# Moving a third of the local product and the last third of the gating to GpSimd, with output sums, scaling and MLP rows one to three rows later

## The chip, the cores and the metric

The kernel runs on one core of one Trainium2 chip. The metric is device time in microseconds (us), the median of three runs. The profile is one execution of the same program, recorded by the hardware profiler. PE is TensorE, DVE is VectorE, ACT is ScalarE, POOL is GpSimd, SP is the engine that only issues DMAs.

## What is computed

Eight samples of 384 channels on a 32 x 32 grid (1024 tokens) go through two layers. Cut to what matters:

```python
# layer 0, per sample
xn    = rmsnorm(x) * norm_w
u, z  = in_proj(xn)                      # mamba, forward and backward in time
u     = silu(causal_conv1d(u))           # 4 taps
dt, B, C = x_proj(u)
delta = softplus(dt_proj(dt))
h     = exp(delta * A) * h + delta * u * B    # scan over 1024 tokens, 16 states
y     = sum_n(h * C) + u * D             # both directions
g     = out_proj(y * silu(z)) * scale_mod
local = sigmoid(depthwise3x3(xn)) * xn
x     = x + res_scale * (g + local)
# layer 1, per sample
t = tokens(x)
t = t + Wo(causal_attention(layernorm(t)))    # 6 heads of 64
t = t + mlp(layernorm(t))                     # 384 -> 1536 -> 384, gelu
```

## The kernel before

Tensors are channel-major: three tiles (k = 0, 1, 2) of 128 channels x 1024 tokens. Layer 0 of sample b and layer 1 of sample b-1 are worked in the same iteration b; iterations 1 to 6 are one hardware loop, 0, 7 and 8 are written out. Iteration 8 has layer 1 alone.

**The head of an iteration.** PE makes the forward causal convolution in six halves (`causal`, L555), ACT applies SiLU to each half (`silu_u`, L895) between making the taps of the depthwise convolution for tile 2 (`tap_row_of`, L942 and L949; `TAPS` says how many taps come ahead of each SiLU), and POOL adds those taps (`depthwise`, L1495). DVE does the depthwise convolution of tiles 0 and 1 (L1268, L1272). PE then projects to dt, B and C (`steps_in`, L567), ACT copies the result out (`narrow_copies`, L855 and L856) and PE projects the step sizes (`step_size`, L603). ACT takes the three sigmoids (`gates`, L931, order `BRANCH` = tiles 0, 2, 1), DVE multiplies each by xn and `rs_col` (`local`, L1280), ACT does softplus (L868, L872, L876), DVE finishes it (L1239) and multiplies by u (L1256). POOL multiplies y by silu(z) of sample b-1, three tiles (`gated`, L1502), and PE's `out_project` (L512) waits for all three. Then PE makes z (`in_project`, L531).

**The rows.** 96 rows follow (r = 0 to 95: 2 directions x 16 states x 3 tiles). For each, POOL makes delta*u*B (`input_row`, L1521), ACT the decay (`decay`, L886, one row ahead), DVE the scan (`scan_row`, L1310) and the product with C (`output_row`, L1319), and POOL sums the result into y by an accumulating DMA, two rows later (`sum_row`, L1536). POOL also issues the local products to DRAM behind rows 0 to 2 (`keep_local`, L1507). PE is free of the rows and does the rest of both layers.

**The order of the rest** is written out by hand: `STEPS`, `FINISH`, `BEHIND` and `PLAN` give each item a row, and `SLOTS` collects the items of a row, in the order STEPS, FINISH, SOON, PLAN, rest of BEHIND. Every engine walks the same list and issues its part of each item in row r, in its own program order. On DVE an "early" part stands ahead of the row's scan and the other behind the row; on ACT, around the decay of row r+1. The items of the change are: `wo_add` (DVE adds the attention output to the residual, L1373), `next_*` (norm and input projection of sample b+1: L1144, L1407, L1412, L531, L969), `norm(1)` (L589, L1330, L1024), `mlp_raw` (ACT copies the reduced MLP input out of PSUM, L1106), `mlp_scale` (DVE scales it, L1393), `mlp_cast`, `mlp_split`, `mlp_low`, `mlp_fix` (splitting into bf16 parts, L1109 to L1113, L1396, L1399), `mlp` and `gelu` (four pairs a half, L765, L767, L782, L1121), `mlp_out` (L788, L791), `mlp_add` (ACT, L1134), and `step_silu` (ACT, SiLU of the backward convolution, L909, in row 17, where `PLAN` has attention projection 2, L1046). PE's projection n waits for ACT's copy of projection n-2. `finish` (DVE, rows 0 to 2, two each, L1302) takes the output of `out_project`. After row 95 ACT takes silu(z) of the sample (`silu_z`, L922).

In PE's program the six convolutions of the next head stand behind all items of row 95, so behind `mlp_out`; convolutions 1 to 3 also wait for `mlp_add`.

```python
elif kind == "wo":
    if n >= 2:
        pe.wait_ge(wo_add, at(6, a, n - 1))
```

Of the kernel before, what the change touches and what calls it, by code (L numbers as in the profile page):

```python
# [40 lines left out]
LAG = 2  # L41
TAPS = (0, 3, 3, 4, 5, 6, 6)
BRANCH = (0, 2, 1)
# [34 lines left out]
def norm(n, *rows):  # L78

    return list(zip(("ln_mean", "ln_xc", "ln_var", "ln_rs", "ln_apply"), [n] * 5, rows))  # L80
# [8 lines left out]
def attention():  # L89
# [7 lines left out]
    + [("ctx_t", t, S1 + t // 3) for t in range(6)] + [("wo", t, S1 + (1 if t < 2 else 3)) for t in range(6)]  # L97
    + [("wo_add", t, S1 + 3 + t // 2) for t in range(5)]
    + [("next_square", 0, S1 + 2), ("next_mean", 0, S1 + 2), ("next_rstd", 0, S1 + 4), ("next_norm", 0, S1 + 5), ("wo_add", 5, S1 + 5)]
    + norm(1, S1 + 5, S1 + 6, S1 + 7, S1 + 8)  # L100
    + [("next_in", t, S1 + (6, 8, 10)[t // 2]) for t in range(6)] + [("next_up", t, S1 + (7, 10, 12)[t // 2]) for t in range(6)]
    + [("mlp_in", 0, S1 + 7), ("mlp_raw", 0, S1 + 9), ("mlp_scale", 0, S1 + 10), ("mlp_cast", 0, S1 + 10),
       ("mlp_split", 0, S1 + 10), ("mlp_low", 0, S1 + 11), ("mlp_fix", 0, S1 + 11)] + mlp(0, S1 + 11) + mlp(1, S1 + 21), key=lambda x: x[2])
SOON = [x for x in BEHIND if x[0] in ("step_silu", "step_abs")]
SLOTS = [[(kind, n) for kind, n, row in STEPS + FINISH + SOON + PLAN + [x for x in BEHIND if x not in SOON] if row == r]
# [14 lines left out]
def hybrid_block(nc, x, chan, scal, k128, k32, w_in, w_x, w_dt, w_out, wq, wk, wv, wo, fc1, fc2, pr1, pr2, kept, bc_rows, out):  # L120
    with ExitStack() as ctx:
# [3 lines left out]
        def sem(name):  # L125
            return ctx.enter_context(nc.semaphore(name))
# [52 lines left out]
        def tiled(area):  # L179
# [57 lines left out]

        skip_added = sem("skip_added")
        da_ready, m1_done, scan_done, m2_done = (
            sem(n) for n in ("da_ready", "m1_done", "scan_done", "m2_done"))  # L240
# [255 lines left out]
        def _(pe):  # L496
# [95 lines left out]
            def step_size(b, d, k):  # L592

                g = KT * d + k
                pe.wait_ge(xd_evac, at(4, b, 2 * d + 2))
                if g < 3:
                    pe.wait_ge(m2_done, at(ROWS, b, 0))
                if g == 2:
                    pe.wait_ge(loc_ready, at(KT, b, BRANCH.index(1) + 1))
                if g > KT:  # L600
                    pe.wait_ge(delta_ready, at(6, b, g))
                for c in range(2):
                    mm = pe.matmul(dt_bank[g][:, c * HALF:(c + 1) * HALF], dt_w[d][:, 128 * k:128 * k + 128],  # L603
                                   dtr[d][:, c * HALF:(c + 1) * HALF], start=True, stop=True)
                mm.then_inc(dt_ready, 1)
# [235 lines left out]
        def _(act):  # L841
# [82 lines left out]
            def gates(b, lo, hi):  # L924

                for k in BRANCH[lo:hi]:
                    if k < VK:
                        act.wait_ge(dw_step, at(9 * VK, b, 9 * (k + 1)))
                    else:
                        act.wait_ge(tap_added, at(8, b, 8))  # L930
                    act.activation(taps[k], taps[k], ACT.Sigmoid).then_inc(sig_ready, 1)  # L931

# [217 lines left out]
            def iteration(b, layer0, layer1, more):  # L1150
                if layer0:
# [27 lines left out]
                    for k in range(2):  # L1179
                        skip(b, 0, k)  # L1180
                    for r, d, n, k in rows():
                        for kind, i in beside(r, layer1, more):
                            item(kind, i, b, True)
                        if r + 1 < ROWS:
                            decay(b, r + 1)
                        for kind, i in beside(r, layer1, more):
                            item(kind, i, b, False)
# [10 lines left out]
        def _(dve):  # L1198
# [76 lines left out]
            def local(b, k):  # L1275

                dve.wait_ge(sig_ready, at(KT, b, BRANCH.index(k) + 1))
                for i in range(KT):
# [54 lines left out]
            def item(kind, n, b, early):  # L1333
# [67 lines left out]
                elif kind == "next_norm" and not early:  # L1401
# [7 lines left out]
                    dve.wait_ge(rstd_ready, at(1, b + 1, 1))  # L1409
                    dve.wait_ge(loc_ready, at(3, b + 1, 0))  # L1410
                    for k in range(KT):
# [6 lines left out]
            def iteration(b, layer0, layer1, more):  # L1418
                if layer0:
# [5 lines left out]
                    if b == 0:  # L1425
                        split_hidden()
                    for k in BRANCH:
                        local(b, k)
# [29 lines left out]
        def _(pool):  # L1458
# [37 lines left out]

            def gated(b):

                for k in range(KT):
                    pool.wait_ge(y_in[k], at(YIN, b, YIN))  # L1500
                    pool.wait_ge(zs_ready, at(3, b, k + 1))
                    pool.tensor_tensor(zs[:, k, :], y[:, k, :], zs[:, k, :], ALU.mult).then_inc(yz_ready, 1)  # L1502

            def keep_local(b, k):

                pool.wait_ge(loc_ready, at(KT, b, BRANCH.index(k) + 1))
                pool.dma_start(kept[b][128 * k:128 * k + 128, :], gate[k], accum_op=ALU.add).then_inc(kept_add[k], 16)  # L1507
# [40 lines left out]
            def iteration(b, layer0, layer1, more):  # L1548
                if layer0:
                    depthwise(b)  # L1550
                    if layer1:
                        gated(b - 1)
                    pool.wait_ge(kept_set, at(16, b, 16))
                    for r in range(ROWS):
                        for kind, i in beside(r, layer1, more):
                            item(kind, i, b, more)
                        input_row(b, r)
                        if r < KT:
                            keep_local(b, (1, 0, 2)[r])
# [72 lines left out]
```

## Time and profile before

| | |
|---|---|
| median of three runs | 4047.45 us (4042.24 to 4050.1) |
| the profiled execution's own time | 4031.18 us |
| its span, first to last instruction | 4029.3 us |
| PE busy | 3381.3 us, 84% |
| DVE busy | 3497.5 us, 87% |
| ACT busy | 2597.6 us, 64% |
| POOL busy | 2817.5 us, 70% |
| mean granted TensorE clock | 0.894 of full speed |

The busy shares are means over stages: a head (from the last product of row 95 to the scan of row 0, some 37 us) and the 96 rows have different limits. What a moved item costs is read from the stage where it stands.

### The profile page before, as it was taken

The page shows a single profiled execution, that of the slowest core. Times are in us where ns is not written, and L with a number is a line of the kernel's source. Part 1 is how long each engine was busy: PE and PEld are TensorE (multiplying, and loading weights), DVE is VectorE, ACT ScalarE, POOL GpSimd, SP SyncE. Part 2 cuts the span into 40 slices and gives each one's busy share as a digit, 9 for nine tenths or more (in the row PEclk, how much of TensorE's full clock was granted, in tenths as well). Part 3 has the DMA queues.
Part 4 walks back from the last instruction along what each step waited for, and adds up shares of the span by engine and source line. Part 5 has one row for each costly group of instructions (what it writes and reads, how often), then busy time and mean ns, then how long its engine had stood idle before and what let it go on. Part 6 is the DMA issues. An engine that isn't in the chain of part 4 may idle for free.

```text
span 4029.3 us, 39801 instructions
## 1 busy us (share of the span) xinstructions
PE 3381.3 (84%) x11706; PEld 1712.9 (43%) x11722; DVE 3497.5 (87%) x2671; ACT 2597.6 (64%) x3599; POOL 2817.5 (70%) x1714
## 2 busy tenths in 40 slices
PE   7504589988899898989899888998989898996999
PEld 2101236623374235733366234742357333651473
DVE  6999999999899998999999998999999999999121
ACT  5533567676676757767676766767577666767363
POOL 3889887687866877678866888668776788668000
PEclk8756699989999899988999899988999889997999
DMA  4999797898978988888978988789988889789000
GB/s 105 233 249 247 194 230 181 205 211 217 213 186 194 233 210 191 191 205 212 230 185 200 222 210 213 186 194 227 216 187 192 209 210 223 184 196 229 6 7 16
DMA packets 220548, 770.79 MB, mean 191 GB/s; under 512 B 24908, under 2 KB 40574, under 8 KB 220062
## 3 DMA queue, kind: packets, MB, share of 16 engines
q0 software_dynamic: 113616, 413.71, 53.2%
q1 hardware_dynamic: 106702, 354.32, 26.4%
q8 instruction: 107, 1.75, 0.2%
q14 instruction: 123, 1.01, 0.1%
HBM read 339.60 MB, written 39.85 MB: 94 GB/s over the span
## 4 chain that ended last, share of the span: by engine, by line
PE 43%; DVE 20%; issue 12%; ACT 9%; DMA 9%; POOL 7%; ACTq 0%; DVEq 0%; POOLq 0%
DVE pB L1310 14%; PE pW L711 9%; PE pW L624 9%; DMA y<-hb 9%; POOL hb L1521 5%; PE pW L589 4%; PE pW L512 4%; PE pW L555 3%; PE pW L640 3%; ACT pt L1068 2%; PE pW L567 2%; DVE hb L1319 2%; PE pW L782 1%; PE pW L531 1%; PE pW L739 1%
## 5 line engine op out<-in xcount | busy, mean ns | idle before, releaser
L1310 DVE TENSOR_TENSOR_SCAN pB<-pB,hb 128x1024 f32<-128x1024 f32 x768 | 1757.0, 2288 | 67.4 <-ACT pB L886 59.8
L1536 POOL DMA_DIRECT2D y<-hb x765 | 750.1, 980 | 610.6 <-DVE hb L1319 553.8
L1521 POOL TENSOR_TENSOR hb<-du_f,b_row 128x1024 f32<-128x1024 f32 x384 | 1001.0, 2609 | 128.1 <-DMA y<-hb 72.5
L1521 POOL TENSOR_TENSOR hb<-uc_b,b_row 128x1024 f32<-128x1024 f32 x384 | 993.0, 2587 | 72.8 <-DMA y<-hb 68.8
L1319 DVE TENSOR_TENSOR hb<-pB,c_row 128x1024 f32<-128x1024 f32 x768 | 940.2, 1224 | 45.1 <-DVE pB L1310 0.9
L886 ACT ACTIVATE pB<-delta,vec 128x1024 f32<-128x1024 f32 x384 | 429.1, 1118 | 306.2 <-DVE hb L1319 291.4
L886 ACT ACTIVATE pB<-xres,vec 128x1024 f32<-128x1024 f32 x384 | 428.6, 1119 | 213.3 <-DVE hb L1319 212.6
L711 PE MATMUL pW<-area,pt 128*128 128x64 f32 x3456 | 438.0, 281 | 19.3 <-ACT pt L1068 11.7
L711 PEld LDWEIGHTS pW<-area,pt 128*128 128x128 f32 x3456 | 410.6, 195 | 69.1 <-ACT pt L1068 59.0
L1357 DVE TENSOR_REDUCE stat<-pW 128x1 f32<-128x640 f32 (+7 forms) x361 | 258.6, 753 | 161.9 <-PE pW L627 161.9
L1078 ACT ACTIVATE prob<-pW,stat 128x640 f32<-128x640 f32 (+7 forms) x361 | 266.5, 748 | 27.7 <-DVE stat L1357 27.7
L531 PE MATMUL pW<-area,xn_area 128*128 128x512 f32 x576 | 261.7, 610 | 22.1 <-DVE area L1412 10.0
L1068 ACT COPY pt<-pW 128x512 f32<-128x512 f32 x378 | 216.2, 587 | 81.1 <-PE pW L640 75.7
L624 PE MATMUL pW<-area,v_w 128*128 128x512 f32 (+3 forms) x540 | 223.8, 539 | 45.8 <-ACT prob L1078 28.1
L782 PE MATMUL pW<-du_f,pr_w 128*32 128x512 f32 x384 | 223.5, 730 | 29.2 <-ACT du_f L1121 29.2
L555 PE MATMUL pW<-area,v_w 128*128 128x512 f32 x512 | 235.4, 617 | 12.8 <-ACT uc_b L902 5.0
L640 PE MATMUL pW<-consts,prob 128*128 128x128 f32 x1512 | 227.5, 282 | 16.0 <-ACT xn_area L977 15.4
L977 ACT ACTIVATE xn_area<-pW,stat 128x64 f32<-128x64 f32 x384 | 102.5, 311 | 191.6 <-DVE stat L1368 139.7
L624 PE MATMUL pW<-area,w_ko 128*128 128x512 f32 (+3 forms) x542 | 209.5, 509 | 0.2
L640 PEld LDWEIGHTS pW<-consts,prob 128*128 128x128 f32 x1512 | 164.5, 144 | 105.5 <-issue 100.1
L589 PE MATMUL pW<-area,consts 128*128 128x512 f32 x192 | 90.4, 621 | 137.3 <-ACT area L1140 136.2
L1495 POOL TENSOR_TENSOR prob<-prob,hb 128x1024 f32<-128x1024 f32 x64 | 152.4, 2381 | 62.1 <-ACT hb L949 56.1
(185 smaller groups left out, 4953.9 us busy)
## 6 DMA issues: line engine op xcount, KB each, us to landing
y<-hb POOLq DMA_DIRECT2D x765, 512.0 KB, 7.6
b_row<-bc_rows SPq DMA_DIRECT2D x256, 512.0 KB, 5.8
c_row<-bc_rows SPq DMA_DIRECT2D x256, 512.0 KB, 5.7
du_f<-in_x SPq DMA_DIRECT2D x8, 1536.0 KB, 13.1
kept_residual<-in_x SPq DMA_DIRECT2D x8, 1536.0 KB, 20.8
xres<-kept_residual SPq DMA_DIRECT2D x8, 1536.0 KB, 15.7
out_x<-xa SPq DMA_DIRECT2D x7, 1536.0 KB, 8.5
kept_residual<-hb POOLq DMA_DIRECT2D x16, 512.0 KB, 5.3
```

Source lines behind the costliest of these rows:

```text
L531: mm = pe.matmul(bank, ip_w[:, k, 128 * m:128 * m + 128], xnp[:, k, 1 + 16 * c:17 + 16 * c, 1:1 + WW], start=(k == 0), stop=(k == KT - 1))
L555: mm = pe.matmul(pW[:, 2 + i % 2 if d else (i + 3) % 4, :], cd[m][:, 128 * j:128 * j + 128], up[:, m, off:off + HALF], start=(j == 0), sto ...
L624: pe.matmul(bank[:, lo:hi], q, kT[:, h // 2, lo - c0:hi - c0], start=True, stop=hi != end)
L640: mm = pe.transpose(prob_bank(b, half)[:, 128 * j:128 * j + 128], prob[:, half * HALF + 128 * j:half * HALF + 128 * j + 128], ident)
L711: mm = pe.matmul(value_bank(b, g)[:, DH * t:DH * t + DH], pt[:, col:col + 128], vtok[:, j, DH * h:DH * h + DH], start=(m == 0 and q == 0), ...
L886: act.activation(pBC[r % 2][:, :], delta[d][:, k, :], ACT.Exp, scale=vec[:, k, V_A + n:V_A + n + 1]).then_inc(da_ready, 1)
L1068: act.copy(pt[:, half * HALF:(half + 1) * HALF], prob_bank(b, half)).then_inc(pt_ready, 1)
L1078: ex = act.activation(prob[:, c0:end], scores_bank(b, n)[:, c0:end], ACT.Exp, bias=stat[:, 0, st:st + 1], accum_out=stat[:, 1, st:st + 1])
L1310: dve.tensor_tensor_scan(flow(d, buf), flow(d, buf), flow(d, hb[r % NHB][:, :]), 0.0, ALU.mult, ALU.add).then_inc(scan_done, 1)
L1319: dve.tensor_tensor(hb[r % NHB][:, :], pBC[r % 2][:, :], c_row[g % 2][:, :], ALU.mult)\
L1521: pool.tensor_tensor(hb[r % NHB][:, :], du[d][:, k, :], b_row[g % 2][:, :], ALU.mult)\
L1536: pool.dma_start(y[:, k, :], hb[r % NHB][:, :], accum_op=ALU.add).then_inc(y_in[k], 16)
```

## The change

- One third of the local product moves. ACT's sigmoid of tile 2 signals `gate_ready`, ACT scales it by `rs_col` behind the first two skip products (a new 128 x 1024 Identity), and POOL multiplies it by xn in row 2, ahead of its `keep_local` DMA. DVE does tiles 0 and 1 only.
- One third of the gating moves. POOL gates tiles 0 and 1 where it did, and tile 2 behind `input_row` of row 0.
- Taps and SiLUs: `TAPS` puts two taps ahead of the first SiLU instead of three, and one tap more behind the last.
- `step_silu` leaves `SOON`, so that in row 17 it stands behind attention projection 2.
- Rows: `wo_add` 0 to 5 from rows 64, 64, 65, 65, 66, 66 to 64, 64, 66, 66, 67, 67; `next_norm`, `norm(1)`, `next_in`, `next_up`, `mlp_in` and `mlp_raw` one row later; `mlp_scale` to `mlp_fix` and the first MLP half two rows later; the second MLP half three rows later, so that its last GELU is in row 92, `mlp_out` in 93 and `mlp_add` in 95.

```diff
-TAPS = (0, 3, 3, 4, 5, 6, 6)
+TAPS = (0, 2, 2, 3, 3, 4, 5)
...
-    + [("wo_add", t, S1 + 3 + t // 2) for t in range(5)]
-    + [("next_square", 0, S1 + 2), ("next_mean", 0, S1 + 2), ("next_rstd", 0, S1 + 4), ("next_norm", 0, S1 + 5), ("wo_add", 5, S1 + 5)]
-    + norm(1, S1 + 5, S1 + 6, S1 + 7, S1 + 8)
-    + [("next_in", t, S1 + (6, 8, 10)[t // 2]) for t in range(6)] + [("next_up", t, S1 + (7, 10, 12)[t // 2]) for t in range(6)]
-    + [("mlp_in", 0, S1 + 7), ("mlp_raw", 0, S1 + 9), ("mlp_scale", 0, S1 + 10), ("mlp_cast", 0, S1 + 10),
-       ("mlp_split", 0, S1 + 10), ("mlp_low", 0, S1 + 11), ("mlp_fix", 0, S1 + 11)] + mlp(0, S1 + 11) + mlp(1, S1 + 21), key=lambda x: x[2])
-SOON = [x for x in BEHIND if x[0] in ("step_silu", "step_abs")]
+    + [("wo_add", t, S1 + (3, 3, 5, 5, 6)[t]) for t in range(5)]
+    + [("next_square", 0, S1 + 2), ("next_mean", 0, S1 + 2), ("next_rstd", 0, S1 + 4), ("next_norm", 0, S1 + 6), ("wo_add", 5, S1 + 6)]
+    + norm(1, S1 + 6, S1 + 7, S1 + 8, S1 + 9)
+    + [("next_in", t, S1 + (7, 9, 11)[t // 2]) for t in range(6)] + [("next_up", t, S1 + (8, 11, 13)[t // 2]) for t in range(6)]
+    + [("mlp_in", 0, S1 + 8), ("mlp_raw", 0, S1 + 10), ("mlp_scale", 0, S1 + 12), ("mlp_cast", 0, S1 + 12),
+       ("mlp_split", 0, S1 + 12), ("mlp_low", 0, S1 + 13), ("mlp_fix", 0, S1 + 13)] + mlp(0, S1 + 13) + mlp(1, S1 + 24), key=lambda x: x[2])
+SOON = [x for x in BEHIND if x[0] == "step_abs"]
...
-                    act.activation(taps[k], taps[k], ACT.Sigmoid).then_inc(sig_ready, 1)
+                    act.activation(taps[k], taps[k], ACT.Sigmoid).then_inc(sig_ready if k < VK else gate_ready, 1)
...
                     for k in range(2):
                         skip(b, 0, k)
+                    act.wait_ge(gate_ready, at(1, b, 1))
+                    act.activation(taps[VK], taps[VK], ACT.Identity, scale=rs_col).then_inc(gate_scaled, 1)
...
-                    for k in BRANCH:
+                    for k in range(VK):
                         local(b, k)
...
-            def gated(b):
+            def gated(b, lo, hi):
 
-                for k in range(KT):
+                for k in range(lo, hi):
...
             def keep_local(b, k):
 
-                pool.wait_ge(loc_ready, at(KT, b, BRANCH.index(k) + 1))
+                if k < VK:
+                    pool.wait_ge(loc_ready, at(VK, b, k + 1))
+                else:
+                    pool.wait_ge(gate_scaled, at(1, b, 1))
+                    pool.tensor_tensor(gate[k].rearrange("p (h w) -> p h w", w=WW),
+                                       gate[k].rearrange("p (h w) -> p h w", w=WW),
+                                       xnp[:, k, 1:1 + HH, 1:1 + WW], ALU.mult).then_inc(loc_last, 1)
+                    pool.wait_ge(loc_last, at(1, b, 1))
...
-                        gated(b - 1)
+                        gated(b - 1, 0, 2)
...
                         input_row(b, r)
+                        if r == 0 and layer1:
+                            gated(b - 1, 2, 3)
```

The remaining lines of the diff adapt the counts that `local`, `step_size` and `next_norm` wait for; `next_norm` also waits for `loc_last`, since it overwrites xn.

## Rows read from the trace of the kernel before

**Rows 1.** The chain that ended last, iterations 2 to 3: start, duration, what.

```profile
1359.60 1.46 ACT du_f L1121
...
1371.60 22.58 PE pW L555 x48
...
1394.94 5.37 PE pW L567 x12
```

**Rows 2.** DVE timeline: scans of rows 92 and 95, and of row 0.

```profile
1367.51 2.29 DVE L1310 TENSOR_TENSOR_SCAN pB<-pB,hb 128x1024 f32<-128x1024 f32 x1
...
1377.97 2.29 DVE L1310 TENSOR_TENSOR_SCAN pB<-pB,hb 128x1024 f32<-128x1024 f32 x1
...
1418.54 2.29 DVE L1310 TENSOR_TENSOR_SCAN pB<-pB,hb 128x1024 f32<-128x1024 f32 x1
```

**Rows 3.** ACT timeline: end of iteration 2 and head of 3.

```profile
1371.14 1.44 ACT L1134 COPY xa<-pW 128x1536 f32<-128x1536 f32 x1 [2.39 <-PE pW L791]
...
1400.34 1.00 ACT L855 COPY pt<-pW 32x1024 f32<-32x1024 f32 x1 [3.26 <-PE pW L567]
...
1423.38 1.12 ACT L886 ACTIVATE pB<-delta,vec 128x1024 f32<-128x1024 f32 x1 [1.63 <-DVE delta L1239]
```

**Rows 4.** POOL timeline in the head of iteration 3.

```profile
1405.92 8.01 POOL L1502 TENSOR_TENSOR zs<-y,zs 128x1024 f32<-128x1024 f32 x3
1415.18 2.36 POOL L1521 TENSOR_TENSOR hb<-du_f,b_row 128x1024 f32<-128x1024 f32 x1 [1.25 <-DVE du_f L1256]
```

**Rows 5.** PE timeline: the output projection of iteration 3.

```profile
1414.35 18.41 PE L512 MATMUL pW<-zs,w_qp 128*128 128x512 f32 x36
```

**Rows 6.** Stretches of PE: length, busy and records, granted clock, DMA share, GB/s.

```profile
1418.00:1420.00 2.00, 2.00 (x4) 0.55 0.61 86
```

**Rows 7.** DVE timeline: the first pair of `finish`, iteration 3.

```profile
1424.46 1.40 DVE L1302 SCALAR_TENSOR_TENSOR xa<-pW,tiny,xres 128x512 f32<-128x512 f32 x2
```

**Rows 8.** PE and DVE timelines around rows 17 to 22.

```profile
1485.46 10.46 PE L512 MATMUL pW<-xn_area,w_qp 128*128 128x512 f32 x24
1498.82 4.27 PE L512 MATMUL pW<-xn_area,w_qp 128*128 128x512 f32 x6 [2.90 <-ACT area L1046]
...
1499.81 2.30 DVE L1310 TENSOR_TENSOR_SCAN pB<-pB,hb 128x1024 f32<-128x1024 f32 x1 [1.90 <-ACT pB L886]
...
1516.01 2.30 DVE L1310 TENSOR_TENSOR_SCAN pB<-pB,hb 128x1024 f32<-128x1024 f32 x1 [5.64 <-ACT pB L886]
```

**Rows 9.** DVE timeline: the stall of row 22 in iterations 2 and 6.

```profile
1044.67 2.30 DVE L1310 TENSOR_TENSOR_SCAN pB<-pB,hb 128x1024 f32<-128x1024 f32 x1 [3.86 <-ACT pB L886]
...
2924.03 2.30 DVE L1310 TENSOR_TENSOR_SCAN pB<-pB,hb 128x1024 f32<-128x1024 f32 x1 [6.83 <-ACT pB L886]
```

**Rows 10.** DVE timeline: stalls in the second half of iteration 2.

```profile
1255.90 0.75 DVE L1373 SCALAR_TENSOR_TENSOR xa<-pW,vec,xa 128x512 f32<-128x512 f32 x1 [0.55 <-PE pW L512]
1258.48 0.75 DVE L1373 SCALAR_TENSOR_TENSOR xa<-pW,vec,xa 128x512 f32<-128x512 f32 x1 [1.82 <-PE pW L512]
...
1287.27 0.69 DVE L1393 TENSOR_TENSOR pW<-prob,pW 128x512 f32<-128x512 f32 x1 [1.59 <-ACT prob L1106]
1289.21 0.70 DVE L1393 TENSOR_TENSOR pW<-prob,pW 128x512 f32<-128x512 f32 x1 [1.25 <-ACT prob L1106]
...
1343.12 2.30 DVE L1310 TENSOR_TENSOR_SCAN pB<-pB,hb 128x1024 f32<-128x1024 f32 x1 [1.83 <-ACT pB L886]
```

**Rows 11.** Waits of DVE over the span: us in total, times, longest.

```profile
DVE pB L1310 <- ACT pB L886: 59.8, 29, 6.8
...
DVE pW L1393 <- ACT prob L1106: 19.2, 14, 1.6
```

**Rows 12.** ACT, POOL and PE timelines at the end of iteration 7.

```profile
3718.50 2.95 ACT L922 ACTIVATE zs<-zs 128x1024 f32<-128x1024 f32 x3
...
3719.70 2.36 POOL L1546 TENSOR_TENSOR zs<-y,zs 128x1024 f32<-128x1024 f32 x1 [1.24 <-ACT zs L922]
...
3728.78 15.74 PE L512 MATMUL pW<-zs,w_qp 128*128 128x512 f32 x30 [16.22 <-DVE zs L1293]
```

More of the change, by code:

```diff
@@ L238, in hybrid_block @@
         skip_added = sem("skip_added")
+        gate_ready, gate_scaled, loc_last = sem("gate_ready"), sem("gate_scaled"), sem("loc_last")
         da_ready, m1_done, scan_done, m2_done = (
@@ L598, in step_size @@
                 if g == 2:
-                    pe.wait_ge(loc_ready, at(KT, b, BRANCH.index(1) + 1))
+                    pe.wait_ge(loc_ready, at(VK, b, VK))
                 if g > KT:
@@ L1275, in local @@
             def local(b, k):
-                dve.wait_ge(sig_ready, at(KT, b, BRANCH.index(k) + 1))
+                dve.wait_ge(sig_ready, at(VK, b, k + 1))
                 for i in range(KT):
@@ L1409, in item @@
                     dve.wait_ge(rstd_ready, at(1, b + 1, 1))
-                    dve.wait_ge(loc_ready, at(3, b + 1, 0))
+                    dve.wait_ge(loc_ready, at(VK, b + 1, 0))
+                    dve.wait_ge(loc_last, at(1, b + 1, 0))
                     for k in range(KT):
```

## The prediction

> **What bounds the kernel now.** The page's busy shares are near each other for DVE and PE and name no bound, so I read the chain of waits first, then the timelines of iteration 2 into 3 (the others repeat them), then DVE's waits. In the rows DVE sets the pace: a row takes (1377.97 - 1367.51) / 3 = 3.49 us [rows 2], and moving an item helps there only where it removes a DVE stall. In the head it is otherwise. The chain goes from the last GELU of the MLP through its reduction and `mlp_out` straight into the six convolutions, 22.58 us of PE without a break, then `steps_in`, the copies and softplus [rows 1]. ACT stands idle 3.26 us until `steps_in` ends [rows 3]. So whatever starts the convolutions later makes the head longer by as much, and what starts them is the end of the MLP, since PE's program has them behind it.
>
> **MLP rows.** The last GELU moves from row 89 to 92: three rows, 3 x 3.49, 10.4 us. It stands behind a decay as before, so it starts at 1370.0 instead of 1359.60 and the convolutions at 1382 instead of 1371.60 [rows 1], half a us past the end of row 95 at 1381.5 (its scan from 1377.97, one row long [rows 2]). Nothing on the way has slack, since ACT waited for PE already [rows 3]. ACT gets `mlp_add`, silu(z) and the taps later too; I place its last taps but one at 1410, just when `steps_in` is due. `TAPS` as changed fits that and gives nothing in these heads, where the SiLUs wait for PE. Six heads (2 to 7) follow an iteration with an MLP and convolutions behind it: 6 x 10.4 = **+62.4**. Bounds: 0, if the head had another bound, and 66, if the taps come 0.6 late. In heads 0 and 1 no MLP is in the way and convolution 4 waits for the first SiLU, which now has one tap less ahead of it, about 1.1 us each (the decay of the same shape took 1.12 [rows 3]): **-2**.
>
> At the end of iteration 7 the copy of `mlp_add`, 1.44 us [rows 3], runs after row 95 (3723.0), and silu(z) behind it. With a table load and the first SiLU, 2.4 us, POOL's first gating starts at 3726.9 instead of 3719.70, 7.2 later; from there to `out_project` it was 9.1 us [rows 12]. Some of the 9.1 was DVE's own last product, which no longer waits, so I take **+6**, between 4 and 8.
>
> Late with it is the load of the residual that `finish` reads, issued behind the output store. It has over 30 us in heads 2 to 7 and 15 at the end, and I give it nothing. The Trainium skill, Trainium Kernel Development and Optimization, Key Constraints, says that DMAs issued from the SP, ACT and POOL queues run on the same 16 DMA engines and interleave. By it the store and the load, issued together now, share bandwidth, and the last head could wait some us for them; no row shows the two side by side.
>
> **The later third of the gating.** Three gatings took 8.01 us and ended at 1413.93; `out_project` began at 1414.35. POOL's first input row ended at 1417.54 [rows 4, 5]. The third gating now follows that: 1417.54 + 2.36 = 1419.9, and `out_project` starts 5.55 us later. It makes six results of six records. The first six records run at half clock, to about 1419.8 [rows 6]; the other 30 take (18.41 - 5.45) / 30 = 0.43 each, 2.58 a result. PE stands idle ahead of it, so I assume the same slow start: results at 1425.0, 27.6, 30.2, 32.8, 35.4 and 38.0. DVE took them in pairs, without waiting, at 1424.46 [rows 7] and then every 4.8 us (a row and the pair). Now the second result holds it 2.6 us, and the fourth and sixth about 0.4 each: **3.5** a head, seven heads (1 to 7), **+24.5**. Bounds: nothing, if PE is quick, and 5.55 each, 39 in all. z follows 5.5 us later; its copies in rows 4 to 7 are then just in time.
>
> **The local third.** DVE loses a product of 1.3 us a head, but it waited between these products for ACT, so the chain gains nothing. ACT's new scaling, about 1.1 us, fits ahead of decay 1, where ACT idled 1.63 us [rows 3]; without that gap it would be on the path of row 1, 8 us in all, kept for the range. POOL's new product, 2.36 us by the nearest row [rows 4], comes in row 2. Input rows 3 to 5 come 2 to 3 us later by it, and `sum_row` and the DMAs queued behind it on POOL too; DVE, 3.5 us late, still finds them ready. So 0; if DVE is not late, some 1 us a head.
>
> **`step_silu` behind projection 2.** Four projections run from 1485.46 in 10.46 us, so projection 2 is ready at 1493.3; its copy comes only behind the SiLUs and two table loads, and it is what lets PE go on at 1498.82, slower than before [rows 8]. `steps_in` and the copies that precede the decay of row 22 follow, and DVE stalls 5.64 us. Now the copy comes at 1493.4, ahead of the SiLUs. PE goes on at 1495.9 and reaches `steps_in`'s end some 4.4 us sooner; in exchange the decay of row 19 is 1.0 us later, 0.8 of it ACT waiting for the projection. The stalls 1.90 and 5.64 [rows 8] become 2.9 and 0.4: -4.2 here. The seven stalls of row 22 lie between 3.86 and 6.83 [rows 9] and make 36.2 of the 59.8 in DVE's waits for the decay [rows 11]. Less 7 x 1.0 for row 19 and 7 x 0.4 left: **-26**. Bounds: +7 (only the later decay) and -36.
>
> **Output sums, scaling, second MLP half.** DVE waits 0.55 + 1.82 = 2.37 us for the third and fourth output sum [rows 10], in other iterations 3.6. A row later both are ready; 0.35 is left at `next_norm`. Iterations 1 to 6 together -17, 7 another -1: **-18**. `mlp_scale` waits 1.59 + 1.25 = 2.84 us for ACT's copies [rows 10], 19.2 in all [rows 11]. A row of distance more ends that wait. But `next_up` 2 and 3 now stand ahead of `mlp_cast` on ACT and wait for PE, which starts on them with ACT's copies at 1288.5 and needs 2 x 2.58 us: cast at 1294.3, and `mlp_split` waits for it, 1.4 us. **-10**. The first GELU of the second half stalls DVE by 1.83 us, one row behind `mlp_add` [rows 10]; two rows behind it does not. Five such stalls and small ones of 0.2: **-11**, within the same 59.8 [rows 11]. Bounds for the three: -20 and -52.
>
> **The sum.** 62.4 - 2 + 6 + 24.5 - 26 - 18 - 10 - 11 = **+26 us**. Against the profiled execution (4031.2 us, of which 4029.3 are span) that is 4057. The median of the runs shown is 16 us above it, and I add to the median: 4047.45 + 26 = 4073.5. About 0.2%, 8 us, is what a measurement of this kernel can tell from no change.
>
> **Rivals.**
> - *The row-17 gain does not come*: the backward chain or ACT keeps row 22 late. For: ACT's copies, decays and SiLUs of rows 17 to 21 stand in one queue, and I placed them. Against: both the stall and PE's gap of 2.90 ahead of it are rows [rows 8]. 26 + 26 to 33 = +52 to +59, about 4103.
> - *The later gating costs next to nothing*: 26 - 24.5 = +1.5, and with the sums' and the scaling's waits gone entirely -3; about 4048. For: PE may start faster than I assume. Against: 5.55 us against a slack of 3.
> - *The late MLP is absorbed*, the other side. Place: the start of the convolutions. It decides if the head is not waiting for them: if `steps_in` could end 10 us later and the copies on ACT not move. Then 62.4 and 6 fall away: 26 - 68 = -42, 4005; with half absorbed -8. For: ACT has much other work in the head. Against: ACT's wait of 3.26 us and the chain itself [rows 1, 3].
> - *It doesn't do what it says*: the rows are fixed lists, so little can fail. 0.02.
>
> **Chances.** Forecast (+10 to +42) 0.46; no row-17 gain 0.20; gating free 0.18, half of it within 0.2% and a quarter on each side; MLP absorbed 0.14, of which 0.02 within 0.2%; the last 0.02, within. Faster by over 0.2%: 0.045 + 0.12, about 0.16; within 0.09 + 0.02 + 0.02 = 0.13; slower 0.71. The range, 4042 to 4108, holds the first two cases and most of the third, and leaves out the absorbed one.
>
> **What would show it.** Right: the convolutions of heads 2 to 7 start half a us behind row 95, not 10 us ahead of its end; from the scan of row 95 to that of row 0 it is 40.57 [rows 2] + 10.4 = 51.0; L1302 stands among DVE's waits with about 3.5 us a head; row 22 stalls under 1 us; L1373 and L1393 nearly leave the waits and L1396 enters with 1.4. Wrong: the convolutions start late and the head keeps its length, or stalls appear in rows 82 to 95.

## The result, and the profile after

The changed kernel takes 4058.5 us against 4040.8 for the kernel before (medians of 20 runs each): 17.7 apart. The ratio is 1.0039, interval 1.0031 to 1.0047, so 12.5 to 19 us slower. The forecast was 4073.5, +26 on a median of 4047.45; that median of three runs lay 6.6 us above the one of 20.

The profiled executions lie further apart than the medians: spans 4029.3 and 4061.4 us, 32 apart. That of before took 4031.2 us, 9.6 below the median of its kernel; that of after took 4063.2, 4.7 above the median of its own. So 14 of the 32 us come from which executions were profiled. Part of it has a place: in three iterations of before rows 17 to 23 take 26.8 us, where the five runs below that leave `step_silu` in place need 28.4 or more in 34 of 35 iterations, and 5 to 9 us more over seven. All differences of segments below are against that trace of before.

The page of after, its head and busy times:

```profile
span 4061.4 us, 39821 instructions
...
PE 3389.5 (83%) x11722; PEld 1716.3 (42%) x11722; DVE 3481.0 (86%) x2663; ACT 2605.6 (64%) x3607; POOL 2835.6 (70%) x1722
```

DVE has 16 us less work, POOL 18 more, ACT 8 more, and the mean granted clock is 0.886 instead of 0.894. None of these shares tells the sign. The waits of DVE do (us in total, times, longest):

```profile
DVE hb L1283 <- ACT pB L932: 88.9, 15, 16.5
DVE xa L1305 <- PE pW L513: 42.5, 33, 8.9
...
DVE xa L1376 <- PE pW L513: 21.0, 7, 11.1
DVE pB L1313 <- ACT pB L887: 18.1, 16, 1.5
DVE pB L1313 <- POOL hb L1532: 16.1, 25, 2.1
...
DVE pW L1399 <- ACT pt L1110: 1.5, 6, 0.3
```

(L1283, L1305, L1313, L1376 and L1399 were L1280, L1302, L1310, L1373 and L1396. Of L1376's 21.0 all but 0.8 lie in iteration 8, which has no rows.) The wait for the decay fell from 59.8 to 18.1 and L1393's 19.2 left the list [rows 11]. In exchange DVE waits 88.9 us for the first sigmoid of a head, 14.9 before, and 42.5 for `out_project`, 13.6 before. With the starts of the 768 scans in DVE's timeline the span falls into segments; this table sums them (us, after minus before):

| segment | change | term of the prediction |
|---|---|---|
| heads 2 to 7 | +58.4 | MLP late, +62.4 |
| head 1 | -1.4 | taps, -2 with head 0 |
| rows 0 to 3, iterations 1 to 7 | +32.4 | later gating, +24.5 |
| rows 17 to 23 | -37.1 | `step_silu`, -26 |
| rows 23 to 33 | +8.7 | none |
| rows 61 to 76 | -32.2 | sums and scaling, -28, and part of the next |
| rows 76 to 87 | -10.1 | second MLP half, -11 |
| behind the last scan | +7.1 | +6 |
| iteration 0 and other rows | +6.3 | 0 |

**The head.** ACT's timeline of iteration 2 into 3 (start, duration, what, idle ahead and its releaser):

```profile
1372.25 1.45 ACT L1122 ACTIVATE du_f<-pW 128x1536 f32<-128x1536 f32 x1
...
1383.68 1.44 ACT L1135 COPY xa<-pW 128x1536 f32<-128x1536 f32 x1 [3.95 <-PE pW L792]
...
1412.32 1.00 ACT L856 COPY pt<-pW 32x1024 f32<-32x1024 f32 x1 [0.80 <-PE pW L568]
```

PE's timeline, the same head:

```profile
1380.81 2.84 PE L792 MATMUL pW<-narrow,mixed 32*128 32x512 f32 x6
1383.58 15.70 PE L556 MATMUL pW<-area,v_w 128*128 128x512 f32 x32
1399.12 7.03 PE L556 MATMUL pW<-area,w_ko 128*128 128x512 f32 x16
1406.92 5.36 PE L568 MATMUL pW<-area,xp_w 128*56 128x512 f32 x12 [0.78 <-ACT area L896]
```

and DVE's:

```profile
1380.35 2.29 DVE L1313 TENSOR_TENSOR_SCAN pB<-pB,hb 128x1024 f32<-128x1024 f32 x1
...
1417.87 1.28 DVE L1283 SCALAR_TENSOR_TENSOR hb<-pB,tiny,area 128x1024 f32<-128x1024 f32 x1 [10.28 <-ACT pB L932]
...
1428.97 1.75 DVE L1259 TENSOR_TENSOR du_f<-delta,area 128x1024 f32<-128x1024 f32 x1
1430.64 2.28 DVE L1313 TENSOR_TENSOR_SCAN pB<-pB,hb 128x1024 f32<-128x1024 f32 x1
...
1438.63 0.75 DVE L1305 SCALAR_TENSOR_TENSOR xa<-pW,tiny,xres 128x512 f32<-128x512 f32 x1 [1.39 <-PE pW L513]
1441.21 0.75 DVE L1305 SCALAR_TENSOR_TENSOR xa<-pW,tiny,xres 128x512 f32<-128x512 f32 x1 [1.82 <-PE pW L513]
```

Count from the scan of row 95. The last GELU stands 8.1 us ahead of it (8.0 predicted), the convolutions start 3.2 behind it (4.0 predicted; before, they started 6.4 ahead of it [rows 1, 2]), and row 0 follows at 1430.64 - 1380.35 = 50.29 us (51.0 predicted). In this head everything behind the convolutions moved rigidly: they are 9.6 us later and row 0 is 9.7 later. ACT's wait for `steps_in` shrank from 3.26 [rows 3] to 0.80, since its last taps but one came late as well, but PE's `steps_in` still ended it.

Over heads 2 to 7 the convolutions start 10.6 us later on the mean, and the way from them to row 0 is 0.9 shorter, 46.5 us for 47.3; together they make the 58.4. The time was won mostly in heads 5 and 7. There, before, the convolutions had started 8.9 us or more ahead of the scan of row 95, and PE stood still among them for 1.2 and 2.4 us, waiting for ACT's SiLU (L895). Row 0 came 48.8 and 50.0 us behind their start; in the changed kernel, where nothing interrupts them, it is 46.7 and 46.6.

**The gating.** POOL's timeline in the same head:

```profile
1427.28 2.35 POOL L1532 TENSOR_TENSOR hb<-du_f,b_row 128x1024 f32<-128x1024 f32 x1 [4.73 <-DVE du_f L1259]
1429.59 3.33 POOL L1506 TENSOR_TENSOR zs<-y,zs 128x1024 f32<-128x1024 f32 x1
```

PE's timeline, the output projection behind it:

```profile
1433.16 18.30 PE L513 MATMUL pW<-zs,w_qp 128*128 128x512 f32 x36 [6.88 <-POOL zs L1506]
```

The stretches of its start (length, busy and records, granted clock, DMA share, GB/s):

```profile
1433.00:1435.00 2.00, 1.84 (x2) 0.50 0.47 39
1435.00:1437.00 2.00, 2.00 (x4) 0.50 0.97 182
1437.00:1439.00 2.00, 2.00 (x4) 0.64 1.00 143
1439.00:1449.00 10.00, 10.00 (x25) 1.00 0.91 186
```

After 6.88 us of idleness PE starts at a granted clock of 0.50, the lower level, 1.2 GHz, as assumed. The kernel before started this projection without idling, and the clock stood no higher:

```profile
1414.00:1416.00 2.00, 2.00 (x3) 0.50 0.00 0
1416.00:1418.00 2.00, 2.00 (x4) 0.50 0.00 0
```

The first result is there 5.5 us after the start, the next 2.58 later. DVE stalls 1.39 us for the first, 1.82 for the second and 0.28 each for the fourth and the sixth; the prediction had 2.6 for the first pair and 0.4 each. The third gating took 3.33 us, not 2.36; `out_project` starts 2.52 us behind the scan of row 0, where before it started 4.19 ahead [rows 2, 5]: 6.7 later, not 5.55.

The seven heads have 25.6 us of these stalls, 3.7 each, close to the 3.5 predicted. The rest of the +32.4 is mostly work that got longer. In row 0 DVE's third product of delta and u now runs beside POOL's input row of row 1, which the late gating pushed there, and takes 1.82 us (1.47 in iteration 1) where it took 1.22; a pair of finishes, now taken singly, takes 0.1 us more:

```profile
1435.42 1.82 DVE L1259 TENSOR_TENSOR du_f<-delta,area 128x1024 f32<-128x1024 f32 x1
```

**Row 17.** ACT's timeline in iteration 3; the first line is its copy of attention projection 2:

```profile
1508.84 0.67 ACT L1047 ACTIVATE area<-pW,tiny 128x512 f32<-128x512 f32 x1
1509.52 1.28 ACT L910 ACT_TABLE_LOAD   x1
1510.82 2.95 ACT L910 ACTIVATE uc_b<-uc_b 128x1024 f32<-128x1024 f32 x3
1513.78 1.28 ACT L1002 ACT_TABLE_LOAD   x1
1515.08 1.12 ACT L887 ACTIVATE pB<-delta,vec 128x1024 f32<-128x1024 f32 x1
```

PE's timeline there:

```profile
1500.75 11.75 PE L513 MATMUL pW<-xn_area,w_qp 128*128 128x512 f32 x27
1513.82 5.36 PE L568 MATMUL pW<-uc_b,xp_w 128*56 128x512 f32 x12 [1.32 <-ACT uc_b L910]
```

DVE's scan of row 19:

```profile
1516.23 2.30 DVE L1313 TENSOR_TENSOR_SCAN pB<-pB,hb 128x1024 f32<-128x1024 f32 x1 [1.49 <-ACT pB L887]
```

The 5.64 us of row 22 are gone, in all seven iterations, and the stall of row 19 fell from 1.90 [rows 8] to 1.49, where 2.9 was expected (over seven iterations from 11.8 to 10.4 us).

### The profile page after: what moved, and what is told of

The parts are those of the page before. It is cut to its first block, busy times and chain, and to the rows that moved or that the text cites. A ratio compares the mean times of both kernels' runs of the same rounds, so it can differ in the third digit from the quotient of the medians.

```text
span 4061.4 us, 39821 instructions
## 1 busy us (share of the span) xinstructions
PE 3389.5 (83%) x11722; PEld 1716.3 (42%) x11722; DVE 3481.0 (86%) x2663; ACT 2605.6 (64%) x3607; POOL 2835.6 (70%) x1722
## 3 DMA queue, kind: packets, MB, share of 16 engines
q0 software_dynamic: 113616, 413.71, 52.8%
q8 instruction: 106, 1.74, 0.2%
## 4 chain that ended last, share of the span: by engine, by line
PE 46%; DVE 23%; issue 12%; ACT 8%; POOL 6%; DMA 5%; ACTq 0%; DVEq 0%; POOLq 0%
DVE pB L1313 17%; PE pW L712 10%; PE pW L625 9%; PE pW L513 7%; DMA y<-hb 5%; PE pW L556 4%; POOL hb L1532 4%; PE pW L590 3%; PE pW L641 3%; ACT pt L1069 2%; PE pW L532 2%; DVE hb L1322 2%; PE pW L568 1%; PE pW L783 1%; PE pW L604 1%
## 5 line engine op out<-in xcount | busy, mean ns | idle before, releaser
L1313 DVE TENSOR_TENSOR_SCAN pB<-pB,hb 128x1024 f32<-128x1024 f32 x768 | 1757.1, 2288 | 34.9 <-ACT pB L887 18.1
L1532 POOL TENSOR_TENSOR hb<-du_f,b_row 128x1024 f32<-128x1024 f32 x384 | 1013.1, 2640 | 98.5 <-DVE du_f L1259 45.3
L1079 ACT ACTIVATE prob<-pW,stat 128x640 f32<-128x640 f32 (+7 forms) x361 | 266.1, 747 | 27.7 <-DVE stat L1360 27.7
L625 PE MATMUL pW<-area,v_w 128*128 128x512 f32 (+3 forms) x540 | 226.8, 545 | 37.6 <-ACT prob L1079 25.6
```

The lines of the kernel that those rows point to most:

```text
L625: pe.matmul(bank[:, lo:hi], q, kT[:, h // 2, lo - c0:hi - c0], start=True, stop=hi != end)
L1313: dve.tensor_tensor_scan(flow(d, buf), flow(d, buf), flow(d, hb[r % NHB][:, :]), 0.0, ALU.mult, ALU.add).then_inc(scan_done, 1)
L1532: pool.tensor_tensor(hb[r % NHB][:, :], du[d][:, k, :], b_row[g % 2][:, :], ALU.mult)\
```

## The experiments

All ratios are to the kernel before. Where us stand beside a ratio, they are the ratio's difference from 1 times 4040.8.

### The rows: late MLP alone, all rows alone, all but the rows

```diff
# e1_late_half: before, with
-    ... + mlp(0, S1 + 11) + mlp(1, S1 + 21)
+    ... + mlp(0, S1 + 11) + mlp(1, S1 + 24)
# e5_rows_only: before, with the whole PLAN of after
# e4_rows_back: after, with the whole PLAN of before
```

> The kernel before with one edit: the second half of the MLP starts at row 85 instead of 82 (last GELU in row 92). Theory A (the end of the MLP starts the convolutions, and the head waits for them): heads 2 to 7 are 10 us longer, the end of iteration 7 is 6 us longer, and the first GELU of the second half no longer stalls DVE (-10 us): +52 to +58 us, ratio about 1.013 to 1.014. Theory B (the late MLP is absorbed by other work of the head): heads as before, 0 to -10 us, ratio 0.998 to 1.000.

> The kernel before with all row moves of the plan and nothing else. Theory A (the late second half costs what it did alone, and the sums and the scaling give back their waits): +51 from the late half, -17 to -24 from the sums and the scaling, that is +27 to +34 us, ratio 1.0067 to 1.0085, as the difference of the changed kernel and the rows-back one (28). Theory B (the parts work on each other): below +15 or above +45.

> The changed kernel with the rows of the plan (output sums, norm, scaling, MLP) as they were before; gating, local third, taps and the SiLU behind projection 2 stay. Theory A (the late end of the MLP is the loss of the change): against the kernel before, later gating +24 to +32, row 17 -26 to -37: -10 to +5 us, ratio 0.997 to 1.001, so 15 to 25 us faster than the changed kernel. Theory B (the rows pay for themselves): slower than the changed kernel, +20 us or more against the kernel before.

The late second half alone: ratio 1.0126 (1.0107 to 1.0145), +51 us, one below the 52 to 58 of Theory A, with the interval across it. Heads 2 to 7 grow by 52.8, the end by 4.7, and rows 76 to 87 give 8.3 back. Among DVE's waits, behind the attention's line, stands now:

```profile
DVE hb L1280 <- ACT pB L931: 65.8, 7, 12.1
```

All rows alone: 1.0059 (1.0045 to 1.0072), +24 (18 to 29); Theory A had 27 to 34. Heads 2 to 7 +53.1, end +7.1, rows 61 to 87 -42.8. The other way round, after with the old rows: 0.9977 (0.9967 to 0.9987), below the kernel before, and 25 us below after by the ratios, 27.7 by the medians. So the rows cost 24 to 28 us; the prediction's row terms make 62.4 + 6 - 18 - 10 - 11 = 29.4. The convolutions do wait for the end of the MLP, and the rival in which the late MLP is absorbed is refuted.

### The gating: alone, taken back, and behind the products

```diff
# e2_late_gating: before, with gated(b, lo, hi) as in after, and
-                        gated(b - 1)
+                        gated(b - 1, 0, 2)
...
                         input_row(b, r)
+                        if r == 0 and layer1:
+                            gated(b - 1, 2, 3)
# e7_gating_back: after, with these lines undone
# e10_gating_waits: e2_late_gating, with
                         if r == 0 and layer1:
+                            pool.wait_ge(du_ready, at(6, b, 2))
                             gated(b - 1, 2, 3)
```

> The kernel before with one edit: POOL gates the third tile behind the first input row. Theory A (out_project is late by the third gating plus the input row): DVE waits at the finishes, 3.5 us a head by the prediction's placing, 4.6 by the trace after, in seven heads: +24 to +32 us, ratio 1.006 to 1.008. Theory B (part of the 4.6 us of rows 0 to 3 comes from POOL's new product and not from the gating): +10 to +20 us.

> The kernel after, with all three gatings back in the head of the iteration; the late rows, step_silu behind projection 2 and the local third stay. Theory A (every term of the prediction stands on its own wait, so they add): the kernel before with late gating alone lost 33 us, the kernel after with the rows back lost 25 us by its late gating, so this gains 25 to 33 on the kernel after: 4026 to 4034, ratio to the kernel before 0.996 to 0.998. Rows 0 to 3 take 16.8 us again, the finish line's wait for out_project is back to some 14 us in all, the heads 2 to 7 stay at 48 to 51 us. Theory B (late MLP and late gating overlap in the head, so that each hides part of the other): under 15 us of gain, 4044 or more. Theory C (they make each other worse): over 40 us of gain, under 4018.

> The later gating alone, with one more wait: POOL's third gating waits for DVE's second product of delta and u, and so cannot run beside it. Theory A (3.33 us of that gating instead of 2.36 is the two instructions keeping each other from SBUF): the third gating takes 2.36 us, starts about 1 us later and ends when it did, so the time is that of the later gating alone, 4074, within 5 us. Theory B (the 3.33 us have another cause, such as the DMAs in flight): the gating still takes 3.3 us, ends 1 us later and the kernel is 6 to 7 us slower, 4080.

Alone: 1.0087 (1.0070 to 1.0104), +35 (28 to 42), above the 24 to 32 of Theory A. Rows 0 to 3 grow by 27.5, the predicted place, and rows 23 to 33 by 11: there DVE waits 14.7 us for ACT's softplus (L876), against 4.0 before. Taken back from after: 0.9985 (0.9975 to 0.9995), 22 us below after by the ratios, 25.8 by the medians (4032.7), at the edge of Theory A. There rows 0 to 3 shrink by 32.0, while rows 3 to 17 grow by 6.0, of which below.

The third run asks why the gating takes 3.33 us. It lets it wait until DVE's second product of delta and u is done. POOL's timeline about the scan of row 0 in iteration 4, with the late gating alone (e2):

```profile
1903.82 2.35 POOL L1521 TENSOR_TENSOR hb<-du_f,b_row 128x1024 f32<-128x1024 f32 x1 [3.22 <-DVE du_f L1256]
1906.13 3.33 POOL L1502 TENSOR_TENSOR zs<-y,zs 128x1024 f32<-128x1024 f32 x1
```

The same with the wait (e10):

```profile
1916.06 2.34 POOL L1502 TENSOR_TENSOR zs<-y,zs 128x1024 f32<-128x1024 f32 x1 [1.16 <-DVE du_f L1256]
```

DVE's timeline beside them in e2:

```profile
1905.52 1.74 DVE L1256 TENSOR_TENSOR du_f<-delta,area 128x1024 f32<-128x1024 f32 x1
1907.18 2.29 DVE L1310 TENSOR_TENSOR_SCAN pB<-pB,hb 128x1024 f32<-128x1024 f32 x1
```

The gating takes 3.33 where it starts beside that product, and 2.34 where it runs wholly beside the scan, in all seven iterations. The product itself takes 1.22 to 1.23 us alone; here it starts beside POOL's input row, which ends at 1906.2, and takes 1.74. The numbers are those of two instructions that take turns: the product ends 1.1 us after POOL's gating has started, and 1.1 + 2.34 is 0.1 more than 3.33. The Trainium skill, SBUF — State Buffer, Who interferes with whom, says this: a VectorE instruction with two SBUF inputs and a GpSimd instruction that reads SBUF exclude each other, and the second waits until the first is done, while a VectorE instruction with one SBUF input, outside its two-port modes, leaves GpSimd alone (the scan has one, its other is in PSUM). The trace agrees, 3.33 against 2.34. Had the prediction taken it into account, it would have added some 1 us a head.

The kernel did not gain by that wait: 1.0097 (1.0081 to 1.0113), at or above the one without it; the intervals overlap. Its median, 4083.1, lies outside Theory A's 4074 within 5. Counted from the scan of row 0 the two gatings end within 0.3 us of each other (2.3 and 2.5 us behind its start), so nothing could be won. Between the two traces rows 0 to 3 grew by 5.5 us, in two parts. DVE's third product of delta and u takes 2.03 us in place of 1.82, 1.5 in all. The stalls for `out_project` make 24.8 in place of 20.8: PE's clock rose later after its start. The stretches of PE, first two to four us behind the start of `out_project` in e2 (iteration 4), then two to six us behind it in e10 (iteration 3):

```profile
1911.70:1913.70 2.00, 2.00 (x5) 0.73 0.98 195
```

```profile
1441.86:1443.86 2.00, 2.00 (x4) 0.50 1.05 199
1443.86:1445.86 2.00, 2.00 (x4) 0.58 0.96 117
```

In e2 the first result came 4.2 to 4.8 us behind the start in five of seven heads, in e10 5.2 to 5.5 in five of seven. The heads are 7.0 us longer in all as well; why is open.

### `step_silu` behind projection 2

```diff
# e3_silu_behind: before, with
-SOON = [x for x in BEHIND if x[0] in ("step_silu", "step_abs")]
+SOON = [x for x in BEHIND if x[0] == "step_abs"]
```

> The kernel before with one edit: the SiLU of the backward convolution stands behind attention projection 2 in row 17. Theory A (the copy of projection 2 was what held up PE and with it row 22): rows 17 to 23 are 4 to 7 us shorter in iterations 1 to 7, of which rows 23 to 33 give back about 1.2 us each: -26 to -37 us, ratio 0.991 to 0.994. Theory B (the stall moves on to the softplus in rows 24 to 30 whole): 0 to -8 us, ratio 0.998 to 1.000.

0.9920 (0.9903 to 0.9938), -32 us (25 to 39). Rows 17 to 23 shrink by 35.5, rows 23 to 33 grow by 7.1, of which 5.9 are waits for POOL's input rows. Both are against the one trace of before, and its stalls of row 22 are small: 36.2 us in seven iterations, where the five other traces that leave `step_silu` in place, each with another edit, have 41.8 to 44.8. In iteration 2, for example, before has 3.86 [rows 9], and DVE's timeline of e1, whose edit lies in later rows, has:

```profile
1055.92 2.30 DVE L1310 TENSOR_TENSOR_SCAN pB<-pB,hb 128x1024 f32<-128x1024 f32 x1 [5.30 <-ACT pB L886]
```

DVE's timeline of e3 in iteration 3 shows both changes: the stall of row 22 is gone, that of row 19 is 1.49, and POOL's input rows are late in rows 27 and 29, where the kernel before has no stall.

```profile
1495.89 2.30 DVE L1310 TENSOR_TENSOR_SCAN pB<-pB,hb 128x1024 f32<-128x1024 f32 x1 [1.49 <-ACT pB L886]
...
1526.86 2.30 DVE L1310 TENSOR_TENSOR_SCAN pB<-pB,hb 128x1024 f32<-128x1024 f32 x1 [0.52 <-POOL hb L1521]
...
1536.87 2.30 DVE L1310 TENSOR_TENSOR_SCAN pB<-pB,hb 128x1024 f32<-128x1024 f32 x1 [0.52 <-POOL hb L1521]
```

### The local third

```diff
# e8_local_only: before, with the diff of keep_local, local, gates and the scaling alone
# e9_no_rows_no_gating: e4_rows_back, with the lines of e2_late_gating undone
# e11_silu_taps: e3_silu_behind, with
-TAPS = (0, 3, 3, 4, 5, 6, 6)
+TAPS = (0, 2, 2, 3, 3, 4, 5)
```

> The kernel before with only the local third moved: ACT scales, POOL multiplies in row 2, DVE does two products. Theory A (DVE waited for ACT between its products, so nothing is gained, and ACT's and POOL's new work is covered): 0 us, ratio 0.999 to 1.001. Theory B (DVE's 1.3 us a head is on the path, as the two edits measured alone add up to +1 and the rows-back kernel came out at -10): -8 to -10 us, ratio 0.9975. Theory C (POOL's product delays input rows): +5 to +8.

> The changed kernel without its two losses: plan rows as before, all three gatings where they were. Left of the change: the SiLU behind projection 2, the local third on POOL, the taps. Theory A (the losses are the late end of the MLP and the late gating alone, each by what it measured by itself): the rows-back kernel 4031 less 33: about 3998 us, ratio 0.989 to 0.992, at least as fast as the SiLU edit alone (4008). Theory B (local third and taps cost something themselves): slower than 4008, ratio above 0.993.

> The kernel before with step_silu behind projection 2 and with the taps of the change, nothing else: no local third on POOL and ACT, no late gating, the rows as before. It differs from the earlier version without rows and without late gating (ratio 0.991) only by the local third. Theory A (the local third costs and brings nothing on the path, as predicted): 0.991, 4003 to 4008. Rival B (the third costs some us, as the run with it alone hinted with 5.7 us inside its interval): 0.989 to 0.990, 3998 to 4002. Rival C (the third brings something once step_silu is out of the way, since DVE has one product less in the head): 0.993, 4012 or more. Rows 17 to 23 take 22.5 to 24 us in each.

Alone: 1.0009 (0.9998 to 1.0020), no difference that can be told, with 0.8 us more in rows 3 to 17 of each iteration (5.6 in all). The version with `step_silu`, taps and local third: 0.9909 (0.9894 to 0.9925). The same without the third: 0.9908 (0.9893 to 0.9924), 4002 us. The step from e3 to e11, the taps, is 5 us by the ratios, within their intervals. The pair e9 and e11 says that the third brings nothing and costs at most a few us: rows 3 to 17 are 4.1 longer with it. There POOL's product of row 2 makes its next input rows late, as in this row of DVE's timeline (iteration 3 of e9, row 6):

```profile
1442.30 2.30 DVE L1313 TENSOR_TENSOR_SCAN pB<-pB,hb 128x1024 f32<-128x1024 f32 x1 [0.41 <-POOL hb L1532]
```

With the late gating in place, DVE comes 4 to 5 us later to these rows, and the growth is 0.0. e9 and e11 beat both the kernel before and the one after; of the whole change, the order of row 17 is worth having.

### The rows' gains without their price

```diff
# e12_sums_late: e9_no_rows_no_gating, with the PLAN of after up to mlp_raw, and
-    mlp_scale, mlp_cast, mlp_split S1 + 10; mlp_low, mlp_fix S1 + 11; mlp(0, S1 + 11) + mlp(1, S1 + 21)
+    mlp_scale, mlp_cast, mlp_split S1 + 11; mlp_low, mlp_fix S1 + 12; mlp(0, S1 + 12) + mlp(1, S1 + 21)
# e13_rows_less_two: e9_no_rows_no_gating, with the PLAN of after, but
-    mlp(0, S1 + 13) + mlp(1, S1 + 24)
+    mlp(0, S1 + 13) + mlp(1, S1 + 22)
```

> The version without rows and without late gating, with the output sums a row later (as in the change), what hangs on them and the first MLP half one row later, the scaling one row behind its copies as before, and the second MLP half where it was before (first GELU in row 83). So it takes the sums' part of the change without its price. Theory A (the sums' waits are the gain of rows 61 to 76, 3.3 us in each of iterations 1 to 6, and only the end of the MLP carries the cost): 18 us below that version (4006), 3988, ratio 0.987; rows 61 to 76 take 71 us instead of 74.4, the heads 2 to 7 stay at 38 to 43 us. Rival B (what is won there is lost in the rows behind it or in the head, because PE has its work later and the queue of the MLP closes up): within 6 us of that version, 4000 to 4010, with rows 76 to 95 or the heads longer by about 3 us. Rival C: the first half, one row later beside an unmoved second half, delays the MLP's end as well: heads 3 us longer, 4006.

> The version without late gating but with all rows of the change, except that the second MLP half starts two rows earlier (its last GELU in row 90, one row later than before the change, not three). Theory A (each row of the MLP's end costs one row, 3.49 us a head, and the waits won in rows 61 to 87 stay won): against the version with the rows of before (4006): sums, scaling and second half give 5.0 + 1.9 us in each of six iterations, about 40; the end costs 6 x 3.5 + 2 = 23; so 3989, ratio 0.987; the heads 2 to 7 take 42 to 45 us. Rival B (the head starts late only when the last GELU falls behind some row, since up to 1.5 us of slack exist): heads 38 to 42 us, 3970 or less. Rival C (the rows' gains and the head's loss come as a pair, since PE ends its work of the iteration at the same time whatever the rows): 4006 or more.

0.9920 (0.9904 to 0.9935) and 0.9926 (0.9911 to 0.9942): neither is faster than the version they start from, and the 3988 and 3989 of Theory A are refuted. Segments here are against the trace of e9. In e12 rows 61 to 76 give 18.1 us, as Theory A has it, and the heads do not grow, but rows 76 to 87 take 22.7 more. The place is row 85, whose waits for the decay make 29.5 us in seven iterations, where e9 has 5.9; DVE's timeline of e12 in iteration 3:

```profile
1805.48 2.30 DVE L1313 TENSOR_TENSOR_SCAN pB<-pB,hb 128x1024 f32<-128x1024 f32 x1 [3.37 <-ACT pB L887]
```

PE's timeline ahead of it:

```profile
1798.76 0.60 PE L768 MATMUL pW<-pt,fc_bf 64*128 64x512 bf16 x1 [2.14 <-ACT xa L1135]
```

ACT's timeline:

```profile
1796.66 1.44 ACT L1135 COPY xa<-pW 128x1536 f32<-128x1536 f32 x1 [0.70 <-PE pW L792]
1798.12 1.28 ACT L1122 ACT_TABLE_LOAD   x1
1801.56 1.45 ACT L1122 ACTIVATE du_f<-pW 128x1536 f32<-128x1536 f32 x1 [2.16 <-PE pW L768]
```

PE's first product of the second half waits for `mlp_add` of the first, now a row later and directly ahead of that half's first GELU, and this GELU, waiting for PE, holds ACT's decay. So Rival B holds: the halves are tied, and the gain of the sums moves to row 85. In e13 rows 61 to 76 give 28, rows 76 to 87 take 14 (row 86 waits 21.1 us for the decay) and the heads 12 (2 us each, not 3.5). Its time is Rival C's, 4006 or more, but the loss that cancels the gain lies half in row 86 and not in the head alone.

## Why the prediction was right or wrong

**The direction and its mechanism were right.** The end of the MLP starts the convolutions, three rows later cost nearly three rows a head, and this is more than all the rows' gains: +58.4 against 62.4 in six heads, the end +7.1 against +6, rows 61 to 87 -42.3 against -39. Taken alone the rows cost 24 to 28 us where the terms gave 29.4. Head 1, where the taps count, gave 1.4.

**The size was wrong: +17.7 (12.5 to 19) in place of +26.** The step that failed is the term of `step_silu`, -26, mis-sized. Three runs lie on a way from before to after, and each step has a term:

| step | measured, by the ratios | term |
|---|---|---|
| before to e11: `step_silu` and taps | -37 (-43 to -30) | -26 - 2 = -28 |
| e11 to e9: the local third | 0 | 0 |
| e9 to e4: the later gating | +27 | +24.5 |
| e4 to after: the rows | +25 | +29.4 |

The steps make +16, which is the ratio's 1.0039. The other way round, with e7 in place of e4, the rows take +31 and the gating +22. So gating and rows come out within 5 us of their terms, on either side, and the first step misses its own by 9 us; the interval excludes -28, and so does that of e9. `step_silu` alone is -32 (e3); its interval, 25 to 39, just takes in the 26, and how much of the -37 is the taps' is not told apart.

Two things were wrong in the term. First, it was read from one trace: 36.2 us of row 22 [rows 9, 11], where five other traces have 41.8 to 44.8. Second, it left 7 x 0.4 us in row 22 and added 7 x 1.0 in row 19. Row 22 has no stall left, and row 19 has 10.4 us where it had 11.8. The prediction had the decay of row 19 one us later, "0.8 of it ACT waiting for the projection". ACT does not wait: PE, no longer held by the copy, made 27 records in one go and projection 2 was ready before ACT came to it. One copy more now stands ahead of the SiLUs and one less, 0.7 us, between them and the decay. Against it stands a loss in rows 23 to 33 that the prediction did not name: POOL's input rows are late there, 5.9 us of waits where before had none. With 44 in place of 36.2, no rest in the two rows and some 6 lost behind them the term comes to about -38; this is an estimate from the traces.

**The later gating**, +24.5, measured 22 to 27 in the changed kernel, but its parts were not those predicted. The gating itself was 1 us slower, beside DVE's product. The stalls it made were 25.6 us, and rows 0 to 3 grew by 32.4, since DVE's own work beside POOL got longer. (By the prediction's own numbers, 1419.9 + 5.45, the first result was due at 1425.35 and not at 1425.0.) The late DVE then hid the local third's 6 us in rows 3 to 17. Alone, with nothing to hide, it costs 35, of which 11 lie in rows 23 to 33. That loss is not the one of e3 in the same rows: here DVE waits for ACT's softplus, there for POOL's input rows. With both edits in, the softplus waits are 5.9 us in place of 14.7; how the one edit relieves the other is not shown.

The single effects, 24 + 35 - 32 + 4 = +31, or +26 with the taps, are more than the 17.7. Each has an interval of 4 to 7 us to either side, so that this gap is at the edge of what the runs can tell.

**The local third** cost nothing, as predicted, and "some 1 us a head if DVE is not late" is what e7, e8 and e9 show, 0.6 to 0.9.

**The base** was the other error. The forecast added its sum to a median of three runs, 6.6 us high, and read its costs from a trace that is 10 us faster than the median of 20. The second spoils a sum of differences too, where the stall to be removed is one of those that the fast execution had short, as that of row 22 was. It also hides in a comparison of two profiles: 32 us there, 17.7 in the medians.

**The rivals.** "No row-17 gain" is refuted by e3, "gating free" by e2 and e7, "MLP absorbed" by e1. The signs asked for came: the convolutions' start, 50.3 us for a head, L1305's wait in every head (3.7 us each), row 22 without a stall, L1373 and L1393 without a wait in iterations 1 to 6. L1396 of before entered with 1.5 us in all, where 1.4 a head was expected. `mlp_split` thus waits for almost nothing, and the scaling's gain is whole. The load of the residual, which the prediction gave nothing, made no wait: L1305 waits for PE alone.

## What to carry to other kernels

Where one engine's program puts the head of the next iteration behind the tail of this one, a gain in the middle that is bought with a later tail is paid for at the head, here with 9.7 us for three rows of 3.49; look first at what the tail releases. Items of a hand-written order that wait for each other, as the second MLP half for `mlp_add` of the first, have to move together (e12). A stall that differs from iteration to iteration should be read from several executions before it becomes a term. And ask of each stall removed which wait is the next in the same rows, and of each instruction moved to GpSimd which two-input VectorE instruction runs beside it.

## What the runs showed of the hardware

- GpSimd's product of 128 x 1024 f32 took 2.34 to 2.36 us alone or beside a scan that has one operand in PSUM, and 3.33 us where it started beside VectorE's product of two SBUF tensors; that product took 1.22 to 1.23 us alone and 1.74 to 2.36 beside GpSimd.
- The product of the local third took 2.19 us on GpSimd, against 1.44 on VectorE, which scaled it as well. With the gating in its old place it made the next input rows late (rows 3 to 17, 4 to 6 us in seven iterations); with the late gating it left no trace.
- TensorE started its output projection at the lower level (granted clock 0.50) whether it had idled 6.88 us ahead of it (after, iteration 3) or not at all (before, iteration 3). In the changed kernel the first result of six records took 5.5 us there, the following 2.58 each. In e2, e4 and e10 the first took 4.2 to 5.5 us, less where the clock rose sooner after the start.
